# Temporal rotation in turned weight sets, and half of each normalisation on ScalarE, in a four-layer attention block

## What is computed

```python
def attention(x, w_qkv, w_out, b_out):           # x: [sequences, n, 128], 8 heads of 16
    q, k, v = split(x @ w_qkv)                   # each to heads
    q, k = rotary(q), rotary(k)                  # x * cos + x_rot * sin; x_rot swaps neighbours: (-x2, x1)
    return softmax(q @ k.T * 0.25) @ v @ w_out + b_out

x = ln(x_input)
for i in range(4):
    x_s = attention(layernorm(x as [32, 64, 128]), ...)          # n = 64 patches
    x_t = attention(layernorm((x + x_s) as [128, 16, 128]), ...) # n = 16 times
    x = layernorm(x_s + x_t) + x
x = x_input + x
out = x + moe(ln(x))                             # 8 experts, top 2, each 128 -> 512 -> 128, gelu
```

## Time and profile before

| | before |
|---|---|
| median of 3 runs | 720.98 us (718.01 to 722.47) |
| profiled execution, its time | 720.79 us |
| profiled execution, its span | 719.0 us |
| busy: PE, DVE, ACT, POOL | 506.9, 520.2, 282.7, 252.0 us |
| mean granted TensorE clock | 0.829 of 2.4 GHz |
| chain that ended last: DVE, PE, issue, POOL, ACT | 40%, 34%, 12%, 5%, 5% |

### The profile page before, as it was taken

The page is one execution under the profiler, slowest core; times in us unless marked ns, Lnnn a source line. Parts: engine busy times, 40 slices in busy tenths (PEclk is TensorE's granted clock), DMA queues, the critical chain, the costliest instruction groups (busy, mean ns, idle before and its releaser), DMA issues.

```text
span 719.0 us, 20553 instructions
## 1 busy us (share of the span) xinstructions
PE 506.9 (71%) x8574; PEld 407.7 (57%) x8574; DVE 520.2 (72%) x1484; ACT 282.7 (39%) x436; POOL 252.0 (35%) x197
## 2 busy tenths in 40 slices
PE   0587586678778667877696776776866535898992
PEld 0374564547547545564475446645645524898992
DVE  6869857979896678798956887998479754544444
ACT  0452742174365232653643246436424313333430
POOL 6413502340162221402702313145023072477652
PEclk9889889679985895699768869997898585899996
DMA  3000008400000100000001000000000013033314
GB/s 118 1 2 1 2 3 294 146 2 16 1 2 3 32 1 3 2 16 1 2 3 30 3 2 2 17 1 2 3 2 3 1 45 102 28 91 102 107 34 136
DMA packets 17134, 24.53 MB, mean 34 GB/s; under 512 B 2546, under 2 KB 11892, under 8 KB 16980
## 3 DMA queue, kind: packets, MB, share of 16 engines
q1 hardware_dynamic: 14548, 18.04, 8.0%
q0 software_dynamic: 2496, 5.18, 2.1%
HBM read 16.99 MB, written 9.33 MB: 37 GB/s over the span
## 4 chain that ended last, share of the span: by engine, by line
DVE 40%; PE 34%; issue 12%; POOL 5%; ACT 5%; DMA 2%; DVEq 0%; SPq 0%; POOLq 0%; ACTq 0%
PE turn L612 8%; PE small L722 6%; DVE stats L846 5%; PE score L692 5%; DVE rope L952 5%; DVE rope L942 5%; PE score L812 5%; PE small L824 5%; DVE prob L973 3%; DVE top L971 3%; PE score L667 3%; POOL rstd L450 3%; DVE x_res L923 2%; DVE x_nrm L894 2%; DVE mv L877 2%
## 5 line engine op out<-in xcount | busy, mean ns | idle before, releaser
L562 ACT ACTIVATE probT<-turn 128x512 f32<-128x512 f32 x96 | 53.8, 595 | 112.0 <-PE turn L612 111.8
L450 POOL TENSOR_TENSOR rstd<-veps,mhalf 128x8 f32<-128x8 f32 x28 | 46.4, 1656 | 145.6 <-DVE veps L881 145.1
L971 DVE TENSOR_REDUCE top<-score 128x16 f32<-128x1024 f32 (+1 forms) x48 | 58.5, 1220 | 41.4 <-PE score L692 41.3
L692 PE MATMUL score<-kE,qT 32*32 32x64 f32 (+1 forms) x3072 | 66.5, 291 | 28.2 <-POOL kR L461 12.1
L461 POOL TENSOR_TENSOR kR<-rope,rope 128x512 f32<-128x512 f32 x32 | 43.8, 1369 | 117.5 <-DVE rope L942 117.5
L692 PEld LDWEIGHTS score<-kE,qT 32*32 32x32 f32 (+1 forms) x3072 | 56.6, 140 | 42.4 <-issue 28.9
L612 PE MATMUL turn<-ident,prob 128*128 128x128 f32 x384 | 69.9, 342 | 14.1 <-ACT prob L556 13.7
L480 POOL TENSOR_TENSOR x_bias<-x_res,vec 128x1024 f32<-128x1024 f32 x16 | 37.4, 2351 | 108.1 <-DVE x_mid L999 108.1
L612 PEld LDWEIGHTS turn<-ident,prob 128*128 128x128 f32 x384 | 56.3, 177 | 19.3 <-ACT prob L556 16.6
L973 DVE TENSOR_TENSOR prob<-score,top 128x1024 f32<-128x1024 f32 x48 | 58.8, 1224 | 1.6
L549 ACT ACTIVATE kE<-kR,hmask 128x512 f32<-128x512 f32 x64 | 42.0, 713 | 40.2 <-POOL kR L461 40.1
(11 more groups left out here) (114 smaller groups left out, 962.7 us busy)
## 6 DMA issues: line engine op xcount, KB each, us to landing
w_all<-in_w SPq DMA_DIRECT2D x2, 2048.0 KB, 19.9
dispatched<-in_slots_init SPq DMA_DIRECT2D x2, 1518.0 KB, 9.9
slots<-dispatched SPq DMA_DIRECT2D x6, 396.0 KB, 4.5
pairs<-answers SPq DMA_DIRECT2D x8, 256.0 KB, 3.8
ws<-in_w_s SPq DMA_DIRECT2D x4, 257.0 KB, 2.8
wt<-in_w_t SPq DMA_DIRECT2D x4, 257.0 KB, 2.6
x_in<-in_x SPq DMA_DIRECT2D x2, 512.0 KB, 4.4
vec<-in_vec_in SPq DMA_DIRECT2D x4, 256.0 KB, 3.8
```

What stands on the lines that cost most here:

```text
L450: nc.gpsimd.tensor_tensor(rstd[:, q.nth % 4, :], veps[:, q.nth % 4, :], mhalf[:, :], ALU.pow).then_inc(rstd_ready, 1)
L562: nc.scalar.activation(probT[:, q.nth % 2, 2 * k:2 * k + 2, 2 * h:2 * h + 2, :].rearrange("p k g n -> p k (g n)"), turn[:, u % 2, :].rearr ...
L692: last = nc.tensor.matmul(score[b * n:(b + 1) * n, g, c * 2 * n:(c + 1) * 2 * n], qT[rows, tok:tok + n], kE[rows, :, tok:tok + n], start=q ...
L971: nc.vector.tensor_reduce(tops, mine, AX_X, ALU.max).then_inc(top_ready, 1)
```

## The change

It does five things.

1. **Temporal rotation in the weights.** A new step `spin` comes four times in each layer, with two matmuls of 128x512 each (PE): keys' and queries' weights times a constant table `angles` (1 MB, 16 matrices of 128x128). ACT copies the results into `turned_w`, 2 x 16 weight sets of 128x128. `project` of kind t is now 32 matmuls, one for each of keys and queries and each time, with its own weight set and the 64 tokens of that time (a view of `xnT` in steps of 16 elements). DVE and POOL do nothing for it any more; ACT (step part) reads the four banks and writes `kE` and `qT` back in the order (patch, time).
2. **Half of each normalisation on ScalarE.** In normal of kinds s, t and e DVE does four chunks instead of eight and one small instruction more (`shift` = -mean times rstd), and ACT does the other four as `rstd * x + shift`. The first tile's transposes wait for DVE (`nrm_ready`), the second's for ACT (`nrm_late`). Results go to `x_mid` in place of `x_nrm`.
3. **Memory.** `w2_all`, the experts' second weights, now shares its place with `v_t`, which is used to the end of the last layer, so its 2 MB are loaded after the last `mix` and the first tick waits for them.
4. **New lists** for all engines, with a list of its own for the last layer in TAIL.
5. One load less before the first instruction (the small table `cs_t` is gone).

```diff
-ARENA = (53760 + 16384) // 4
+ARENA = (53760 + 16384 + 17408) // 4
...
 ORDERS = {
     "PE": """
-        head.t10- score.s00 mix.t10- score.s01 out.t10- head.s00 mix.s00 head.s01 mix.s01 out.s00 turn.s10
+        head.t10- score.s00 mix.t10- out.t10- score.s01 head.s00 spin.t00 spin.t01 spin.t02 spin.t03 mix.s00
...
+        w2_all = at("w2_all", [P, EXPERTS, FF], 70144)
...
             for n in range(DEPTH):
...
                 sp.dma_start(wt[:, :], w_t[n]).then_inc(wt_loaded, 16)
+                if n == 0:
+                    sp.dma_start(angles[:, :, :], spin_in).then_inc(spin_loaded, 16)
...
-                    sp.dma_start(w2_all[:, :, :], w2.rearrange("e p n -> p e n")).then_inc(w_loaded, 16)
...
+            sp.wait_ge(small_full, STEPS["mix", DEPTH - 1, T, 1, 0].smalls + 4)
+            sp.dma_start(w2_all[:, :, :], w2.rearrange("e p n -> p e n")).then_inc(w2_loaded, 16)
             fetch(0)
...
         @block.scalar
...
+                if q.step == "spin":
+                    for z in range(2):
+                        u = q.turns + z
+                        act.wait_ge(turn_full, u + 1)
+                        nc.scalar.activation(flat(turned_w[:, z, 4 * q.group:4 * q.group + 4, :]), turn[:, u % 2, :],
+                                             ACT.Copy).then_inc(turn_free[u % 2], 1)
+                elif q.step == "normal":
...
+                    act.wait_ge(shift_ready, late_count(("normal", q.layer, q.kind, q.half, 0)))
+                    for c in range(HC // 2, HC):
+                        k = q.half * HC + c
+                        last = nc.scalar.activation(dst[:, k, 0:P], src[:, k, :], ACT.Identity,
+                                                    bias=shift[:, shift_row(q.kind, q.half), c:c + 1],
+                                                    scale=rstd[:, stat.nth % 4, c:c + 1])
+                    last.then_inc(nrm_late, 1)
...
+                elif q.step == "part" and q.kind == T:
...
+                    for t8 in range(2):
+                        act.wait_ge(spun_full, spun + t8 + 1)
+                        src = score[:, t8, :].rearrange("d (t p) -> d p t", p=PATCH)
+                        for e in range(2):
+                            last = nc.scalar.activation(in_order(kE[:, e, :], t8), src, ACT.Copy, scale=hmask[:, e:e + 1])
+                        last.then_inc(spun_free, 1)
+                    for t8 in range(2):
+                        act.wait_ge(spun_full, spun + 2 + t8 + 1)
+                        src = score[:, 2 + t8, :].rearrange("d (t p) -> d p t", p=PATCH)
+                        nc.scalar.activation(in_order(qT, t8), src, ACT.Copy).then_inc(spun_free, 1)
...
         @block.tensor
...
+                    for z, off in enumerate((WK, WQ)):
+                        u = q.turns + z
+                        if u >= 2:
+                            wait_read(pe, turn_free, u - 2)
+                        nc.tensor.matmul(turn[:, u % 2, :], wt[:, off:off + P], flat(angles[:, 4 * q.group:4 * q.group + 4, :]),
+                                         start=True, stop=True).then_inc(turn_full, 1)
...
+                    if q.kind == T:
...
+                        by_time = xnT[:, q.half * HT:(q.half + 1) * HT].rearrange("d (p t) -> d t p", t=TIME)
+                        for z in range(2):
+                            for t in range(TIME):
+                                last = nc.tensor.matmul(score[:, 2 * z + t // 8, t % 8 * PATCH:(t % 8 + 1) * PATCH],
+                                                        turned_w[:, z, t, :], by_time[:, t, :], start=True, stop=True)
+                                if t % 8 == 7:
+                                    last.then_inc(spun_full, 1)
+                        continue
...
         @block.vector
...
                     dve.wait_ge(rstd_ready, stat.nth + 1)
-                    for c in range(HC):
+                    if q.kind != C:
+                        nc.vector.scalar_tensor_tensor(
+                            out=shift[:, shift_row(q.kind, q.half), :], in0=mv[:, slot, :, 0], scalar=-1.0,
+                            in1=rstd[:, slot, :], op0=ALU.mult, op1=ALU.mult).then_inc(shift_ready, 1)
+                    for c in range(HC if q.kind == C else HC // 2):
...
+def turning_table():
...
+    table[d, :, d] = cos
+    table[d ^ 1, :, d] = sin
+    return table
```

184 lines of the change are left out of this document (122 added, 62 removed).

## The result

| | before | after |
|---|---|---|
| median beside each other (4 runs each) | 721.13 us | 712.3 us (710.34 to 715.13) |
| profiled execution: time, span | 720.79, 719.0 us | 715.13, 712.8 us |
| mean granted TensorE clock | 0.829 | 0.862 |
| chain that ended last: DVE, PE | 40%, 34% | 27%, 52% |

The ratio is 0.9877, with a 95% interval of 0.9837 to 0.9917; a second measurement of 12 runs gave 0.9921 (0.9895 to 0.9947). Medians are of all runs; ratios leave out runs in a slower state, more than 1.5% above the fastest of the same kernel (one of those 12, two of fill_more's four). The change is faster by about 1%, where 4% was forecast.

A forecast was written before the change was run, and what follows sets the result against it. No engine was full: DVE was nearest, PE close behind, the rest hand-over between in-order lists. Savings of 8.8 us a steady layer, less in layers 0 and 3, with start and tail summed to -31.2 from 720.8: 690 us, range 670 to 714.

The forecast's parts named there:

- (C): From score.s10 to out.s10: -4.7 us a layer, -2.0 from the new order of score.s11 and -2.7 from a better PE clock.
- (E): From out.t00 to the next layer's first scores: -3.0 us, by less normalisation and a projection at a better PE clock.
- the walk: Going through one layer of the new lists with measured durations: -10.3 us, -8.8 after 1.5 for small hand-overs.
- layer 0: First layer: -7.6 us, gaining less in (A) since spin meets PE at half clock with no other half's work to fill.
- What leaves and what comes: Busy time a layer: DVE loses 15.1 us of rotation and 3.3 of normalisation, PE gains 13.4 at full clock, ACT 11.
- (A): From a layer's first scores to out.s00: +5.6 us, spin's 6.8 on half 0's path less 1.2 hidden in PE's wait.
- (B): From out.s00 to score.s10: -1.6 us, DVE's rotation ahead of the scores relieved by project.t00 on PE.
- (D): From out.s10 to out.t00: -6.6 us, rotation -7.5, half normalisation -0.8, divide.t00 ahead of normal.t10 +1.7.
- The tail: After the last layer: +1.5 us counted; the w2 load hidden with 3 us to spare, costing up to some 5 otherwise.
- The half normalisation: Four of eight chunks leave DVE in each normalisation: 3.3 us busy a layer, 0.8 on the path in (D).
- PE gives it back by its clock: Rival: spin or project.t00 at half clock, 6.8 us more each; 714 us or about 705, middle 707, chance 0.15.
- The strided projections are slow: Rival: the new projections' matmuls take 0.43 us instead of 0.214, a projection 13.7; whole 737 us, chance 0.08.

The follow-up runs named there:

- fill_more: The fill_ce kernel plus three unread matmuls ahead of mix.t00 and one ahead of the next project.s00; median 716.71 us, four runs from 704.19 to 721.79.
- spin_once: The changed kernel with spin only in layer 0, later layers using its turned weights; 715.78 us, ratio 0.9943 to the kernel before.
- fill_ce: The changed kernel plus unread 128x512 matmuls in each layer, five ahead of score.s11 and three ahead of score.t10; 705.19 us, ratio 0.9803 to the kernel before.
- head_first: The changed kernel with head.s10 ahead of score.s11 again in TensorE's list; 718.77 us, ratio 0.9975 to the kernel before.
- before_norm: The kernel before plus only the half normalisation (four chunks on ScalarE), with its old lists, rotation and memory; 716.72 us, ratio 0.9926.
- norm_fill: The norm_whole kernel plus one unread 128x512 matmul ahead of project.t00 in layers 1 to 3; 715.95 us, ratio 0.9948 to the kernel before.
- after_5: The changed kernel unaltered, measured a second time in five rounds; 714.06 us, ratio 0.9921 to the kernel before.
- norm_whole: The changed kernel with all eight chunks of each normalisation on VectorE again; 731.0 us, ratio 1.0176 to the kernel before.

## Why the prediction was right or wrong

The forecast of 690 us missed, at 712.3, and with it the size of the gain, 8.7 us in place of 31; the sign held. The range (670 to 714) held by 1.7 us, and the second measurement, 714.06, lies on its edge. What failed are the steps (C) and (E) of the walk, and layer 0, to which both were carried over: of the 25 us of span that are missing, layer 0 has 11.5, layers 1 and 2 10.2 and layer 3 3.4.

**What leaves and what comes** was right in busy time: DVE 437 (445 forecast), PE 547 (560), ACT 337 (335). Terms off by a little: 32 matmuls 7.36 us (6.85), spin's 16 records 7.61 (6.8), a chunk of the normalisation on ScalarE 0.41 us (0.33; four took 1.65).

**(A), (B), (D)** held within 0.8 us in layer 1. But the reading of A as "spin is on the path" did not: spin_once took it away and in layers 1 and 2 nothing came sooner. The path there is VectorE's list from out.t10 to divide.s00, and spin fills the wait for it. The number was right for a wrong reason.

**(C) failed in both terms**, -0.9 for -4.7 in layer 1. "The denser PE before it now should keep the clock for part of it", -2.7: it kept it for score.s10 (1.62 us for 2.92), but the wait of 4.56 us ahead of score.s11 is inside the stretch, and the clock behind it was 0.50 as before. The price was right: with the waits filled, C takes 29.4 and 28.7 us in layers 1 and 2 of fill_ce, 2.5 and 3.1 less than before. The first term, -2.0 for the order, counted the transposes as gone from the path. They only moved behind score.s11: mix.s10 comes 0.6 us later after score.s10 than before, and head_first, with the old order, has the same C.

**(E) failed**, +2.1 for -3.0. I had the projection "at a better clock"; most of it ran at half, 6.04 us for 6.72. And I left out what the new list of DVE does ahead of it: DVE waits 1.75 us for rstd from POOL ahead of the next normal.s00, which soft.t10 had covered, and 0.92 us for score.t10, which has gaps of 2.30 us. Less what the halved normalisation saves, that makes +1.9 of the +2.1. ScalarE's list, named as what ends last, cost nothing against before.

**Layer 0** was +3.9 for -7.6. By stretches: A +6.9, B -1.9, C +2.3, D -6.6, E +3.3. I had taken the C and E of later layers over to it. Before, this layer's C already ran at 1.00 from 87 to 95 us; after, the clock stood at 0.50 from 83 to 95 us. There was little half clock to win there, and some full clock to lose.

**The tail** came out at +0.6 (+1.5): the first tick began at 604.15 and didn't wait for w2; it waited 1.08 us for the slots.

**The half normalisation** was priced as work, 3.3 us busy a layer and 0.8 on the path in D. As work it is worth 2 to 5 us in all (before_norm; norm_fill against the changed kernel), but in the new lists 18.7, since without it project.t00 waits and its clock falls.

**The rivals.** "PE gives it back by its clock" (707) was the right mechanism in the wrong place: spin and project.t00, where I looked for it, ran at full clock in every steady layer of the profiled execution (in after_5 spin took 9.15 us once, behind a wait of 2.12); it fell behind the wait ahead of score.s11 and behind the gaps in score.t00 or mix.s11 and in score.t10. I had the row that shows it, 4.00 of 4 us busy at 0.50, and gave it 0.15 beside a forecast that needed the contrary. "The strided projections are slow" had its price right and its cover missing: the Trainium skill, Advanced Engine Details and Errata, section Memory Cachelines, warns of such a view, and 7.08 against 3.67 us agrees with it. With 64 columns the penalty doesn't show, 7.36 against 7.33 us.

What stays open: why the clock falls behind one wait and not behind a like one (0.87 us in layers 0 and 3 of norm_whole; 1.06 and 1.05 us in head_first and after_5), what the gaps put down to issue are, and what the new order is worth, if anything.

## What to carry to other kernels

Where the granted clock is not 1.00 throughout, price a TensorE step at both levels by what stands ahead of it: a wait of a microsecond may be paid again in what follows, so an edit that shortens another engine's work may be worth nothing, or several times its length. Before moving work between engines, try two or three unread matmuls in each of the longest waits: here that brought 11.7 us to the kernel before, for six lines. More of them are not simply better: with four more a layer, in fill_more, the runs spread from 704 to 722 us. An experiment that comes out at the expected number has not shown its cause until its trace has the time where the edit is; that of head_first had it elsewhere. And work removed in front of a wait, in a list of fixed order, only lengthens the wait.

## What the hardware showed unexpectedly

- The clock can fall to half in the middle of dense work: 1.00 at 212 to 216 us, 0.55 and 0.50 in the next two windows, TensorE busy 4.00 of 4 us in both, behind a wait of 0.87 us (norm_whole). With one matmul in that wait it stayed at full. The same place can go either way: behind a gap of 1.06 us the same 32 matmuls took 12.60 us in head_first, behind one of 1.05 us 7.36 in after_5.
- A matmul whose moving operand steps by 64 bytes takes 1.77 us for 512 columns, a straight one 0.92; with 64 columns and a full weight set each, both take 0.23 us.
- Gaps put down to issue in dense small matmuls (0.77 and 1.53 us in score.t10 of layer 1) stand behind the same matmuls in two executions of the changed kernel, and in head_first. Fillers ahead move them to other matmuls and don't remove them (1.31 us in score.t00 of fill_ce).
